# Rough scores of the last attention: two heads as 64-row products side by side in TensorE's row halves

## The reference, cut to what matters

```python
    def _L3_xattn_ref(x, latents, ln_media_w, ln_media_b, ln_lat_w, ln_lat_b, Wq, Wk, Wv, Wout):
        ...
        H, Dh = (8, 64)
        ...
        sim = jnp.einsum('bhqd,bhfd->bhqf', q * scale, k)
        alphas = jax.nn.softmax(sim, axis=-1)
        out = jnp.einsum('bhqf,bhfd->bhqd', alphas, v)
        out = out.transpose(0, 2, 1, 3).reshape(b, Nz, H * Dh)
        return out @ Wout
```

## Time and profile before

| what | value |
|---|---|
| three timed runs | 1906.08, 1910.02, 1911.91 us, median 1910.02 us |
| profiled execution | span 1915.2 us |
| TensorE matmul busy | 1641.2 us (86% of the span), 9225 instructions |
| VectorE busy | 1092.3 us (57%) |
| ScalarE busy | 898.9 us (47%) |
| GpSimd busy | 837.6 us (44%) |
| maxima of the rough scores (line 2401) | 256 instructions, 163.9 us, 682 ns each |
| TensorE's share of the chain that ended last | 64% |

### The profile page before, as it was taken

The page is one execution under the profiler, slowest core; times in us unless marked ns, Lnnn a source line. Parts: engine busy times, 40 slices in busy tenths (PEclk is TensorE's granted clock), DMA queues, the critical chain, the costliest instruction groups (busy, mean ns, idle before and its releaser), DMA issues.

```text
span 1915.2 us, 26188 instructions
## 1 busy us (share of the span) xinstructions
PE 1641.2 (86%) x9225; PEld 1117.0 (58%) x9225; DVE 1092.3 (57%) x2218; ACT 898.9 (47%) x1454; POOL 837.6 (44%) x754
## 2 busy tenths in 40 slices
PE   5954999969966999965996887999999999997998
PEld 3444999946844333355993665555555654563674
DVE  4762556576967355532446798565656666644335
ACT  2322445513335897823443664555454355431363
POOL 3053211123479454422005464566656666754206
PEclk9776999979987899977998987999999999997999
DMA  9613233030000000062113000000000000012354
GB/s 363 225 55 110 79 138 132 21 118 1 1 22 1 1 6 6 7 279 83 51 43 107 1 1 33 1 1 1 1 0 1 1 1 1 0 54 92 125 166 132
DMA packets 61879, 117.76 MB, mean 61 GB/s; under 512 B 7247, under 2 KB 50499, under 8 KB 59064
## 3 DMA queue, kind: packets, MB, share of 16 engines
q1 hardware_dynamic: 53688, 95.90, 14.3%
q0 software_dynamic: 8064, 20.19, 3.2%
HBM read 72.26 MB, written 44.89 MB: 61 GB/s over the span
## 4 chain that ended last, share of the span: by engine, by line
PE 64%; DVE 14%; POOL 9%; issue 4%; DMA 4%; ACT 4%; SPq 0%; POOLq 0%; DVEq 0%; ACTq 0%
PE psum L166 60%; POOL arena L1839 3%; DMA arena<-xb 2%; DVE arena L2401 2%; POOL arena L870 2%; DVE rounded L2330 2%; DVE arena L1736 1%; POOL xb L1057 1%; DVE arena L171 1%; POOL arena L1856 1%; DVE arena L2473 1%; PE psum L682 1%; DVE arena L1968 1%; ACT arena L1607 1%; DVE arena L187 1%
## 5 line engine op out<-in xcount | busy, mean ns | idle before, releaser
L166 PE MATMUL psum<-arena 128*128 (+16 forms) x5084 | 1029.4, 438 | 115.3 <-DVE arena L1717 20.0
L166 PEld LDWEIGHTS psum<-arena 128*128 128x128 f32 (+4 forms) x5084 | 587.4, 175 | 451.7 <-issue 289.8
L166 PE MATMUL psum<-rounded 128*128 128x256 f32 (+9 forms) x3072 | 535.2, 340 | 5.8 <-ACT rounded L1572 1.4
L166 PEld LDWEIGHTS psum<-rounded 128*128 128x128 f32 (+5 forms) x3072 | 406.5, 186 | 143.0 <-issue 56.1
L2501 POOL TENSOR_TENSOR arena<-arena 128x1024 f32<-128x1024 f32 (+1 forms) x111 | 263.2, 2371 | 130.9 <-ACT arena L2451 127.3
L2401 DVE TENSOR_REDUCE arena<-psum 128x1 f32<-128x512 f32 x256 | 163.9, 682 | 98.3 <-PE psum L166 96.7
L2451 ACT ACTIVATE arena<-psum 128x1024 f32<-128x1024 f32 x144 | 147.4, 1025 | 147.6 <-PE psum L166 146.9
L1607 ACT ACTIVATE arena<-psum,arena 128x1024 f32<-128x1024 f32 x128 | 134.7, 1117 | 24.0 <-PE psum L166 22.5
L870 POOL DMA_INDIRECT arena<-yb,arena x48 | 45.9, 957 | 211.1 <-DMA yb<-arena 197.6
L1210 POOL DMA_INDIRECT yt<-arena x40 | 39.8, 996 | 182.8 <-DVE arena L1173 177.3
L918 DVE SCALAR_TENSOR_TENSOR rounded<-arena,rounded 128x540 fp32r<-128x540 f32 (+1 forms) x96 | 81.9, 886 | 33.4 <-ACT rounded L1119 32.3
(11 more groups left out here) (266 smaller groups left out, 1905.5 us busy)
## 6 DMA issues: line engine op xcount, KB each, us to landing
arena<-in_w SPq DMA_DIRECT2D x8, 2048.0 KB, 8.4
arena<-xb SPq DMA_DIRECT2D x70, 128.0 KB, 2.3
yb<-arena SPq DMA_DIRECT2D x70, 128.0 KB, 1.8
arena<-in_w1u SPq DMA_DIRECT2D x4, 2048.0 KB, 14.5
xb<-arena SPq DMA_DIRECT2D x3, 2048.0 KB, 16.0
xb<-arena SPq DMA_DIRECT2D x2, 2064.0 KB, 31.5
arena<-xb SPq DMA_DIRECT2D x8, 516.0 KB
yt<-arena SPq DMA_DIRECT2D x2, 2048.0 KB, 15.6
```

What stands on the lines that cost most here:

```text
L166: return e.matmul(o, l, r, start=start, stop=stop, skip_group_check=True)
```

## The change

The rough score of a head now uses only the high parts of its queries, which lie in 64 partitions: `x3_Q1[high3(a), ...]` times `x3_K1[high3(a), ...]`. The two heads lie in different row halves of the array. One item is now both heads' matmuls of the same query block and key block, issued one behind the other, into two banks (bk and bk + 1). VectorE takes the maxima of both banks with one instruction. A group has 9 items (8 pairs and item 0) where it had 17, and each step j from 0 to 7 holds one. Item 0 keeps its eight matmuls, now of 64 rows, in two banks. Banks 5 and 6 are one buffer now: an item waits for the maximum of the item just before it. The first group takes turns between banks 2 and 3 and banks 5 and 6. Its early items move: none is left at step 20 of the stage before, one stands at each of steps 21 to 24, and VectorE takes the first at step 22 and the next two at step 23.

```diff
-        ROUGH_EARLY = {20: (0, 1), 21: (2,), 22: (3,), 23: (4, 5), 24: (6, 7)}
-        ROUGH_TAKEN = {21: (0, 1), 22: (2, 3), 23: (4, 5)}
+        ROUGH_EARLY = {20: (), 21: (0,), 22: (1,), 23: (2,), 24: (3,)}
+        ROUGH_TAKEN = {21: (), 22: (0,), 23: (1, 2)}
...
-            return 5 + (17 * G + k) % 2, 17 * G + k
+            return 2 if G == 0 and k % 2 == 0 else 5, 9 * G + k
...
-            elif G:
-                e.wait_ge(s_ar, at - 1)
-            elif at >= 4:
-                e.wait_ge(s_ar, at - 3)
+            if G:
+                e.wait_ge(s_ar, at)
+            elif at >= 2:
+                e.wait_ge(s_ar, at - 1)
...
-                        m = mm(e, psum[:, bk, 128 * t + 64 * a:128 * t + 64 * a + 64],
-                               x3_Q1[:, G % 3, a, 128 * t:128 * t + 128], x3_K1[:, n % 2, a, 1024:1088], True, True)
+                        m = mm(e, psum[:, bk + a, 64 * t:64 * t + 64],
+                               x3_Q1[high3(a), G % 3, a, 128 * t:128 * t + 128], x3_K1[high3(a), n % 2, a, 1024:1088],
+                               True, True)
             else:
-                t, a, c = (i - 1) // 4, (i - 1) // 2 % 2, (i - 1) % 2
-                m = mm(e, psum[:, bk, :], x3_Q1[:, G % 3, a, 128 * t:128 * t + 128],
-                       x3_K1[:, n % 2, a, 512 * c:512 * c + 512], True, True)
+                t, c = (i - 1) // 2, (i - 1) % 2
+                for a in range(2):
+                    m = mm(e, psum[:, bk + a, :], x3_Q1[high3(a), G % 3, a, 128 * t:128 * t + 128],
+                           x3_K1[high3(a), n % 2, a, 512 * c:512 * c + 512], True, True)
...
-                m = e.tensor_reduce(x3_MX[:, t, a, c:c + 1], psum[:, bk, :], AX.X, ALU.max)
+                t, c = (i - 1) // 2, (i - 1) % 2
+                m = e.tensor_reduce(x3_MX[:, t, :, c], psum[:, bk:bk + 2, :], AX.X, ALU.max)
...
                     if j < 8 and G + 1 < 16:
-                        for i in rough_step3(j):
-                            pe_rough3(e, G + 1, i)
+                        pe_rough3(e, G + 1, j + 1)
```

More of the change, by code:

```diff
@@ L2342, in dve_side3 @@
                     dve_stats(e, t)
-        ROUGH_EARLY = {20: (0, 1), 21: (2,), 22: (3,), 23: (4, 5), 24: (6, 7)}
-        ROUGH_TAKEN = {21: (0, 1), 22: (2, 3), 23: (4, 5)}
+        ROUGH_EARLY = {20: (), 21: (0,), 22: (1,), 23: (2,), 24: (3,)}
+        ROUGH_TAKEN = {21: (), 22: (0,), 23: (1, 2)}
         def rough_order3(G):
-            return list(range(17)) if G else [*range(1, 17), 0]
-        def rough_step3(j):
-            return [0] if j == 8 else [2 * j + 1, 2 * j + 2]
+            return list(range(9)) if G else [*range(1, 9), 0]
         def rough3(G, i):
             k = rough_order3(G).index(i)
-            if G == 0:
-                return (2, 5, 3, 6)[k % 4], k
-            return 5 + (17 * G + k) % 2, 17 * G + k
+            return 2 if G == 0 and k % 2 == 0 else 5, 9 * G + k
         def pe_rough3(e, G, i):
             n, (bk, at) = G // 2, rough3(G, i)
-            if at % 17 == 0:
+            if at % 9 == 0:
                 e.wait_ge(s_lo3, SIDE3_LOW["q", G, 0])
                 e.wait_ge(s_mo, SIDE3_KEPT["k", n, 1 if G == 0 else 2])
-            if at == 17:
-                e.wait_ge(s_ar, 17)
-            elif G:
+            if G:
+                e.wait_ge(s_ar, at)
+            elif at >= 2:
                 e.wait_ge(s_ar, at - 1)
-            elif at >= 4:
-                e.wait_ge(s_ar, at - 3)
-            elif at == 1:
+            elif at == 0:
+                e.wait_ge(s_mo, SIDE3_KEPT["v", 0, 0])
+            else:
                 e.wait_ge(s_qk, NT)
-            elif at == 2:
-                e.wait_ge(s_mo, SIDE3_KEPT["v", 0, 0])
-            elif at == 3:
                 e.wait_ge(s_qsc, NT)
@@ L2397, in dve_rough3 @@
             if i == 0:
-                m = e.tensor_reduce(x3_MX[:, :, :, 2], psum[:, bk, :].rearrange("p (t a l) -> p t a l", t=4, a=2), AX.X, ALU.max)
-            else:
-                t, a, c = (i - 1) // 4, (i - 1) // 2 % 2, (i - 1) % 2
-                m = e.tensor_reduce(x3_MX[:, t, a, c:c + 1], psum[:, bk, :], AX.X, ALU.max)
+                m = e.tensor_reduce(x3_MX[:, :, :, 2].rearrange("p t a -> p a t"),
+                                    psum[:, bk:bk + 2, 0:256].rearrange("p a (t l) -> p a t l", t=4), AX.X, ALU.max)
+            else:
+                t, c = (i - 1) // 2, (i - 1) % 2
+                m = e.tensor_reduce(x3_MX[:, t, :, c], psum[:, bk:bk + 2, :], AX.X, ALU.max)
             m.then_inc(s_ar, 1)
         def dve_maxima3(e, G):
-            e.wait_ge(s_ar, 17 * G + 17)
+            e.wait_ge(s_ar, 9 * G + 9)
             settle(e, dve, e.tensor_reduce(x3_M1, x3_MX, AX.X, ALU.max))
@@ L2535, in pe_xattn3 @@
             pe_side3(e, FIRST3[7])
-            for r in rough_order3(0)[8:]:
+            for r in rough_order3(0)[4:]:
                 pe_rough3(e, 0, r)
@@ L2587, in dve_xattn3 @@
             e.memset(x3_NM, 0.0)
-            for i, r in enumerate(rough_order3(0)[6:]):
+            for i, r in enumerate(rough_order3(0)[3:]):
                 dve_rough3(e, 0, r)
-                if i == 4:
+                if i == 2:
                     dve_side3(e, FIRST3[6])
@@ L2603, in dve_xattn3 @@
                     if j < 8 and G + 1 < 16:
-                        for i in rough_step3(j):
-                            dve_rough3(e, G + 1, i)
+                        dve_rough3(e, G + 1, j + 1)
                     if G:
```

## The result

The changed kernel takes 1930.74 us (median of four runs, 1926.23 to 1935.81) against 1910.97 for the kernel before: a ratio of 1.010, 95% interval 1.0074 to 1.0126. That is slower, and beyond the upper end of the range, 1925. The profiled run is the shortest of the four: 1926.23 us, span 1924.4.

What follows compares the result with a forecast made beforehand. The prediction took the stage as bound by TensorE, with pauses in fixed places. Its terms, 2.6 + 1.1 + 0.2 + 1.0 = +4.9 us, gave 1914.9 us; the range was 1908 to 1925.

Steps and rivals of the forecast that it cites:

- the clock falls: Rival: more TensorE gaps halve the granted clock at group ends, 1.56 us each, +11 in all: 1926; chance 0.10.
- the pair of j = 5: Even group, behind the pause for the keys' low parts: maximum -0.08, load and way out +0.19, so +0.11 us.
- Plain step: Step with the pair between score products: 0.32, 0.43 and 0.34, 1.09 against 0.95, so +0.14 us.
- The maximum over two banks: VectorE's one maximum over 1024 columns: 1.21 us against 1.29 for two, -0.08 where it is on the chain.
- The "short" maximum: Rival: the maximum over two banks takes 1.02 us, giving 1909, no change; chance 0.10.
- Two groups: Sum over an even and an odd group of the last attention: +0.37 us, seven times, +2.6.
- The 10.28 us piece: TensorE piece of the even group's chain with the rough items of j = 2 and 3: +0.14 - 0.05 = +0.09 us.
- Item 0: Item at each group's start: 1.07 us after against 1.19 before, -0.12; +0.3 if the halves' loads do not run side by side.
- Group 14: Group without "q", "k" or "v" work: the buffer sets 1.79 us from pair to pair; +1.1 us (0.5 to 1.6).
- The start: First group: pair 3's wait delays the context rows' transposes and GpSimd's fills, which end 1.3 us later; +1.0 us taken.
- the form is not free: Denies the rival that changing form is free, a pair taking 0.24 us in place of 0.48: 1890; chance 0.07.
- the halves do not take turns: Denies the rival that the row halves take turns in this stage, +13 us in all: 1928; chance 0.04.

Runs made afterwards that it cites:

- one-wait kernel: The kernel before, with the first rough product of j = 5 in even groups up to 12 waiting for the maximum just before it: 1918.86 us.
- changed kernel with repeated scores: The changed kernel, with two high score products of j = 5 computed twice in even groups up to 12: 1919.23 us.
- the second: Second profile, from running the changed kernel once more, unaltered: 1928.54 us.
- pairs with two buffers: The kernel before with rough products as pairs of 64 rows, each product keeping its own bank, maximum and wait: 1930.12 us.

## Why the prediction was wrong

**The step that failed** is the rival "the clock falls", put at 0.10. It was set aside because "before, pauses of 0.7 us and the tails leave the clock at 1.00". So the sum has no term for the clock, which took 7.8 us of the 14.1 in the first profile (below). The row shows that the kernel before holds its clock; it doesn't show by how much. The one-wait kernel measures that margin: 0.26 us more behind the pause is already too much in three groups there, and brings two falls at group ends. The forecast itself had put the pair's wait right there ("Behind the pause the pair of j = 5 waits for the maximum") and counted it as +0.11 us. The rival's price was right: 1.56 forecast, 1.5 measured (65.13 - 63.62), and its 1926 is nearer than the forecast. But it looked at the ends of groups, as at 1488.91, and counted seven stretches there; in the changed kernel five lie behind the pause of j = 5, one of them double. That its time comes near is luck in part.

**What the clock cost.** Against the changed kernel with repeated scores the stage is 7.8 us longer (515.6 - 507.8) in the first profile, and 10.8 in the second, which has one stretch more, of twice the length. Set against 507.8, the kernel before has 501.5: 6.3 are left for the rest of the change, where the forecast had 4.9 in all.

**The terms of the sum**, where the clock holds:
- Plain step: right. A pair's two products start 3 ns apart, 0.32 behind the last score product and 0.43 ahead of the next. In order of time, beside the earlier trace rows:

```profile
1358.20 0.82 PE L166 MATMUL psum<-rounded 128*128 128x512 f32 x3
1358.52 0.93 PE L166 MATMUL psum<-rounded 64*128 64x512 f32 x3
1358.95 0.73 PE L166 MATMUL psum<-rounded 128*128 128x512 f32 x2
```

- The maximum over two banks: 1.24 us on the chain, 1.21 forecast. The "short" maximum (1.02) is out.
- Two groups: +0.37 forecast, +0.60 to 0.67 measured. The 10.28 us piece gained 0.16, not 0.09, the odd group's long piece 0.40, not 0.29, and the piece behind the pause 0.22 (4.60 to 4.82), not 0.19; the even group's tail gained less than forecast, 0.06 for each of two maxima.
- Item 0: -0.12 forecast. From the last transpose to the second score product 1.10 us pass, where 1.24 did. The 0.17 and 0.13 us in that term stood in no row; the sum came out.
- Group 14: +1.1 forecast, 25.16 - 23.92 = +1.24 measured, from the last exponential of group 13 to that of group 14. Its 17.67 us piece is broken by the buffer where the forecast had it, pairs 1.82 us apart (1.79 forecast):

```profile
1663.36 2.12 PE psum L166 x14
1665.49 0.02 issue
1665.51 1.24 DVE arena L2395
1666.75 0.04 issue
1666.79 0.52 PE psum L166 x2
1667.31 0.02 issue
1667.33 1.24 DVE arena L2395
1668.57 0.04 issue
1668.61 5.66 PE psum L166 x24
```

- The start: the transposes do wait for pair 3, but the fills end 0.7 us later, not 1.3, and the exponential of j = 5 in the first group 0.4, where +1.0 was forecast (both from the last transposes of step 20). The half-clock stretch over the start, for which the forecast has no term, is 17.1 us long where it was 10.2.
- The other rivals: the form is not free (the pairs with two buffers cost 1.1 us in two groups at full clock), and the halves do not take turns.

**What stays open.** Why the clock falls behind the pause in some groups and not in others with the same order of work is not known. The medians differ by 19.8 us, the stages of the profiles by 14.1 and 17.1, the profiled spans only by 9.2 (1924.4 - 1915.2): the profiled execution of the kernel before, itself 5.2 us above its median, reaches the stage 5.1 us later. The two longer of the four runs, 1932.57 and 1935.81, have a mean granted clock of 0.914 and 0.913, the two shorter 0.917 and 0.919, which would fit more half-clock stretches; no trace of the longer ones exists.

## What to carry to other kernels

A row that shows the full granted clock shows no margin: before adding a wait, or packing products closer, look for places where TensorE already pauses, and price one half-clock stretch there beside the local cost. The test is cheap: repeat a product in the pause; if more work makes the kernel faster, and does nothing where the clock holds, the clock was the loss. Useful work should then be moved there, which here gave 9.9 us to the kernel before and 23 to 24 to the changed one. Packing two products into the row halves doesn't pay here for single pairs between full-array products: 0.32 + 0.43 + 0.34 us stand where 0.95 stood.

## What the hardware showed that was not expected

- 3.3 us of useless products in all (0.47 us in seven places) made the changed kernel 9.3 to 11.5 us faster, and the kernel before no different.
- With less idle time than before, in two groups (2.55 against 3.22 us) and at the pause itself (0.73 against 0.89), TensorE still fell to the 1.2 GHz level when pairs replaced full products.
- Seven moved waits of 0.26 us, 1.8 in all, cost 8.4.
